# Token lists built by bfloat16 one-hot products in place of float32 ones and scatters

## The chip, the cores and the metric

The kernel runs on one core of one Trainium2 chip. The metric is the device time of one execution in microseconds (us), the median of the runs shown. The program is one launch of four stages that follow one another: a selective-scan (Mamba) stage, an attention stage, a routing stage and an expert stage.

## The reference

`x` has 16 sequences of 1,024 tokens of width 256, so 16,384 tokens. A Mamba block and an attention block come first; the last part is a mixture of experts, and it is what the change touches:

```python
probs = jax.nn.softmax(x.astype(jnp.float32) @ router_weight, axis=-1)   # 8 experts
top_p, top_i = jax.lax.top_k(probs, TOP_K)                                # TOP_K = 2
top_p = top_p / jnp.sum(top_p, -1, keepdims=True)
flat_exp = top_i.reshape(-1)
order = jnp.argsort(flat_exp)
...
keep = within < cap                                                       # cap = 5120
...
act = jax.nn.gelu(jnp.einsum('ech,ehf->ecf', exp_in, moe_w1), approximate=False)
exp_out = jnp.einsum('ecf,efh->ech', act, moe_w2).reshape(N_EXP * cap, H)
weighted = exp_out * padded_probs[:, None].astype(exp_out.dtype)
moe = jnp.zeros((N, H), exp_out.dtype).at[padded_ids].add(weighted)
```

Each token goes to its two best experts, and the two results are added to it with the two normalised probabilities as weights.

## The kernel before, in words

**Mamba and attention stages.** They take the first 4,386 us. The attention stage writes two results to DRAM that matter here: `n2`, the normalised rows of all tokens (16,384 rows of 256 float32), which SyncE stores in 64 parts of 256 KB, and `logits`, 8 numbers per token.

**Routing stage** (`routing_stage`, lines 1359 to 1592). Tokens lie as 128 tiles of 128 (one token per partition), so one instruction over all tokens and experts has 128 x 1024 elements. After the softmax, VectorE picks the two best experts as masks `best0` and `best1`, TensorE counts the tokens ahead of each (`within`, `total`), and VectorE makes from this the slot of each of the 256 entries (128 tiles times 2 choices) of each partition. VectorE's instructions up to there are a strict chain: the helper `after_last` makes each wait for the one before. Experts are cut into blocks of 256 slots; there is room for `NB` = 135 blocks, so 34,560 slots in `COLS` = 270 columns of 128 lanes. A slot is thus a lane and a column.

The list that says which token (and with which weight) sits in each slot is made in two ways at once:

- Of the 256 entries, 96 (`BY_POOL`) are scattered by GpSimd to a DRAM list `info` with one indirect DMA each (line 1456), 128 slots at a time. Entries past an expert's capacity get a slot out of bounds (`kept`), and are dropped.
- The other 160 (`BY_MATMUL`) are placed by TensorE. For an entry VectorE makes `hot_lane`, a 128 x 128 float32 matrix with the token number (z = 0) or the weight (z = 1) of partition p at its lane, and `hot_column`, 128 x 270, with a 1 at its column. The product of the two adds the entry into the bank `list_bank`:

```python
for n, (k, tile) in enumerate(BY_MATMUL):
    wait(dve, placed, n - HOT_RING + 1)
    ...
    for z in range(2):
        nc.vector.tensor_scalar(hot_lane[:, at, z], lane_f[:], place[:, k, tile:tile + 1], entry[:, k, tile, z:z + 1],
                                ALU.is_equal, ALU.mult)
    nc.vector.tensor_scalar(hot_column[:, at], column_f[:], column[:, k, tile:tile + 1], None,
                            ALU.is_equal).then_inc(hot, 1)
```

`HOT_RING` = 4 entries may be under way between VectorE and TensorE. When all are placed, ScalarE copies the bank to `made` (line 1467), and the stage ends with a barrier of all engines.

**Expert stage** (`expert_stage`, lines 1595 to 1781). SyncE loads `info` back as `listing`; GpSimd clears `xe` (so that vacant slots hold zeros) and makes the identity `ident`; VectorE adds `made`, and turns vacant slots into row numbers past the end (`token`, lines 1716 to 1728). Then 135 blocks run. For block n, GpSimd gathers 256 rows of `n2` by two indirect DMAs into `xe` (line 1659) and the expert's two weight matrices by two more (line 1651, 1 MB each, rows named by `weight_row`), TensorE transposes the rows (line 1746), multiplies by `w1` (line 1759) and by `w2` (line 1768), ScalarE applies GELU (line 1708), VectorE multiplies with the weight `listing[:, col, 1:2]` (line 1734), and GpSimd adds the rows into `out` by two indirect DMAs (line 1668). Weights and rows are loaded two blocks ahead.

## Time and profile before

| what | value |
| --- | --- |
| median of 3 runs | 6549.09 us (6548.19 to 6552.92) |
| the profiled execution | 6549.9 us |
| its span, first to last instruction | 6548.2 us |
| mean granted TensorE clock over the span | 0.976 of full |
| TensorE matmul busy | 6175.3 us (94%) |
| VectorE busy | 4267.1 us (65%) |
| ScalarE busy | 3519.6 us (54%) |
| GpSimd busy | 5132.0 us (78%) |

The table is of one execution. Busy time is the time in which an engine runs an instruction; it says nothing of whether another engine waits for it. Times of day in the rows further down count from the start of the span, and the granted clock is given as a share of 2.4 GHz.

### The profile page before, as it was taken

To read this page: it belongs to the slowest core of one execution; us is meant where nothing else is said; L and a number is where in the kernel's file an instruction comes from. 1 tells how busy PE (TensorE), PEld (TensorE's weight loads), DVE (VectorE), ACT (ScalarE), POOL (GpSimd) and SP (SyncE) were. 2 spreads that over 40 slices of the span, in tenths; PEclk is the share of its full clock that TensorE was granted. 3 is DMA by queue.
4 is the path that set the end of the run, shared out by engine and by line. 5 is a ranking of instruction groups with operands and counts; after the bars stand their busy time and mean duration, and the time that the engine had idled before them with its cause. 6 is when DMAs were issued, how large, how long until landed. Compare 5 with 4: busy or idle time off the path is not lost. (4 is left out here: it accounts for less than half of the span.)

```text
span 6548.2 us, 78761 instructions
## 1 busy us (share of the span) xinstructions
PE 6175.3 (94%) x25444; PEld 3970.3 (61%) x25444; DVE 4267.1 (65%) x5490; ACT 3519.6 (54%) x6418; POOL 5132.0 (78%) x3926
## 2 busy tenths in 40 slices
PE   7999999999999999999998799978999999999999
PEld 3444444444444444444443588866788888888888
DVE  6999999999999999999999377779100000000000
ACT  5677677767676777676766588750222222222222
POOL 6999999999999999999999677736454545454544
PEclk9999999999999999999999999989999999999999
DMA  3555555555555555555555244330566656566554
GB/s 124 166 162 171 166 168 166 168 165 168 165 172 163 166 165 166 170 164 169 166 163 167 62 121 122 116 120 1 175 190 179 190 179 189 180 189 179 183 162 135
DMA packets 551754, 1029.76 MB, mean 157 GB/s; under 512 B 77426, under 2 KB 245876, under 8 KB 516784
## 3 DMA queue, kind: packets, MB, share of 16 engines
q1 hardware_dynamic: 441168, 669.34, 33.3%
q0 software_dynamic: 110176, 355.39, 18.0%
q8 instruction: 204, 3.34, 0.2%
q14 instruction: 206, 1.69, 0.1%
HBM read 926.04 MB, written 88.72 MB: 155 GB/s over the span
## 5 line engine op out<-in xcount | busy, mean ns | idle before, releaser
L361 POOL TENSOR_TENSOR m_dbu<-m_du,m_bb 128x1024 f32<-128x1024 f32 x1024 | 2390.8, 2363 | 0.0
L739 PE MATMUL m_y_bank<-m_prod,m_ident 128*128 128x512 f32 x4096 | 1977.8, 612 | 143.1 <-POOL m_prod L370 143.1
L512 ACT ACTIVATE m_decay<-m_delta,m_a_neg 128x512 f32<-128x512 f32 x2048 | 1419.4, 695 | 724.7 <-DVE m_h L622 722.7
L739 PEld LDWEIGHTS m_y_bank<-m_prod,m_ident 128*128 128x128 f32 x4096 | 789.2, 196 | 1122.9 <-issue 907.2
L1734 DVE TENSOR_SCALAR e_ye<-e_ybank,e_listing 128x256 f32<-128x256 f32 x270 | 118.2, 479 | 1817.1 <-PE e_ybank L1768 1817.1
L622 DVE TENSOR_TENSOR_SCAN m_h<-m_decay,m_h_end,m_dbu 128x512 f32<-128x512 f32 x1024 | 1259.4, 1267 | 3.4 <-ACT m_decay L512 2.5
L622 DVE TENSOR_TENSOR_SCAN m_h<-m_decay,m_dbu 128x512 f32<-128x512 f32 x1024 | 1197.7, 1207 | 13.8 <-ACT m_decay L512 13.2
L1708 ACT ACTIVATE e_a<-e_ubank 128x512 f32<-128x512 f32 x540 | 322.5, 597 | 1473.6 <-PE e_ubank L1759 1473.6
L370 POOL TENSOR_TENSOR m_prod<-m_h,m_cb 128x1024 f32<-128x1024 f32 x416 | 982.5, 2362 | 20.0 <-issue 15.0
L1759 PE MATMUL e_ubank<-e_xT,e_w 128*128 128x256 f32 x4320 | 978.6, 380 | 1.3 <-ACT e_xT L1699 1.3
L1768 PE MATMUL e_ybank<-e_w,e_a 128*128 128x256 f32 x4320 | 954.5, 379 | 0.7 <-ACT e_a L1708 0.7
L1768 PEld LDWEIGHTS e_ybank<-e_w,e_a 128*128 128x128 f32 x4320 | 820.7, 190 | 112.6 <-ACT e_a L1708 1.1
L1651 POOL DMA_INDIRECT e_w<-in_w,weight_row x270 | 258.3, 957 | 799.0 <-PE e_ybank L1768 734.4
L1759 PEld LDWEIGHTS e_ubank<-e_xT,e_w 128*128 128x128 f32 x4320 | 811.6, 190 | 106.7 <-issue 1.6
L604 DVE TENSOR_TENSOR m_prod<-m_h,m_c_bank 128x1024 f32<-128x1024 f32 x608 | 727.3, 1196 | 42.5 <-ACT m_c_bank L499 22.4
L1668 POOL DMA_INDIRECT out<-e_ye,e_token x270 | 429.2, 1590 | 111.0 <-issue 81.3
L706 PE MATMUL m_side<-m_xnT,m_w_in 128*128 128x512 f32 x1024 | 503.0, 600 | 6.0 <-ACT m_xnT L428 6.0
L711 PE MATMUL m_side<-m_xpad,m_tap_diag 128*128 128x512 f32 x1024 | 495.7, 592 | 0.0
L499 ACT COPY m_c_bank<-m_cv 128x512 f32<-128x512 f32 x608 | 359.3, 591 | 95.3 <-DVE m_prod L604 93.1
L706 PEld LDWEIGHTS m_side<-m_xnT,m_w_in 128*128 128x128 f32 x1024 | 198.9, 195 | 260.3 <-issue 258.1
L1659 POOL DMA_INDIRECT e_xe<-n,e_token x270 | 283.8, 1051 | 85.4 <-issue 82.0
L711 PEld LDWEIGHTS m_side<-m_xpad,m_tap_diag 128*128 128x128 f32 x1024 | 194.3, 190 | 245.3 <-issue 245.3
(216 smaller groups left out, 6663.9 us busy)
## 6 DMA issues: line engine op xcount, KB each, us to landing
m_bb<-rows_bc SPq DMA_DIRECT2D x1024, 256.0 KB, 3.8
m_cv<-rows_bc SPq DMA_DIRECT2D x608, 256.0 KB, 4.0
m_cb<-rows_bc SPq DMA_DIRECT2D x416, 256.0 KB, 3.4
m_xin<-in_x SPq DMA_DIRECT2D x32, 512.0 KB, 5.7
m_xres<-in_x SPq DMA_DIRECT2D x32, 512.0 KB, 5.6
x<-m_xres SPq DMA_DIRECT2D x32, 512.0 KB, 6.3
a_xa<-x SPq DMA_DIRECT2D x64, 256.0 KB, 2.9
a_xr<-x SPq DMA_DIRECT2D x64, 256.0 KB, 3.2
```

Of the source, the lines that this page charges most:

```text
L361: nc.gpsimd.tensor_tensor(dbu[:, slot], du[:, q[1], p * PC:(p + 1) * PC], bb[:, slot].unsqueeze(1).to_broadcast([P, PC, T]), ALU.mult).the ...
L370: nc.gpsimd.tensor_tensor(prod[:, slot], h[:, slot], cb[:, C_BUFFER[k]].unsqueeze(1).to_broadcast([P, PC, T]), ALU.mult).then_inc(prod_by_ ...
L499: nc.scalar.copy(c_bank[:], cv[:, V_BUFFER[k]]).then_inc(c_copied, 1)
L512: nc.scalar.activation(decay[:, cc], delta[:, r, c], ACT.Exp, scale=a_neg[:, c, n:n + 1]).then_inc(decay_done, 1)
L604: nc.vector.tensor_tensor(prod[:, slot], h[:, slot], c_bank[:].unsqueeze(1).to_broadcast([P, PC, T]), ALU.mult).then_inc(prod_by_vector, 1)
L622: nc.vector.tensor_tensor_scan(h[:, slot, cc], decay[:, cc], dbu[:, slot, cc], h_end[:, u, cc:cc + 1] if r else 0.0, ALU.mult, ALU.add).th ...
L706: ins = nc.tensor.matmul(bank, w_in[:, piece, col:col + P], xnT[:, piece], start=(piece == 0), stop=final)
L711: ins = nc.tensor.matmul(bank, tap_diag[:, i, piece], xpad[:, i, piece:piece + T], start=(piece == 0), stop=final)
L739: ins = nc.tensor.matmul(y_bank[:, cc], ident[:], prod[:, slot, cc], start=False, stop=(n == NS - 1))
L1668: nc.gpsimd.indirect_dma_start(out, bass.IndirectOffsetOnAxis(ap=token[:, col:col + 1], axis=0), ye[:, n % Y_RING, j], None, compute_op=AL ...
L1759: ins = nc.tensor.matmul(ubank[:, (n * UG + g) % U_RING, i], w1[:, r, k, c * P:(c + 1) * P], xT[:, n % 2, k], start=(k == 0), stop=(k == K ...
L1768: ins = nc.tensor.matmul(ybank[:, n % 2, j], a[:, n % 2, c, j * P:(j + 1) * P], w2[:, n % W_RING, c], start=(c == 0), stop=(c == FC - 1))
```

## The change

All 256 entries are now placed by TensorE; the scatters, the DRAM list `info`, its clearing and its loading back are gone, and with them `kept` and `made`.

The entries go in 32 groups of 8 (4 tiles, both choices). Per group, VectorE makes 8 lane matrices in one instruction of 128 x 1024 elements in bfloat16 (`hot_lane`, a plain 0 or 1); ScalarE multiplies them by the partition number into `hot_row`; 8 column matrices of 128 x 270 in bfloat16 hold tile + 1 at the column (`hot_column`), and are made by VectorE in even groups and by GpSimd in odd ones. TensorE multiplies each column matrix by both, 16 products per group. One result is the tile + 1, the other the partition number times tile + 1, and VectorE gets the token number from them in 7 instructions after the last product. A ring of 4 groups lies between the engines.

The weights of the list are gone. `n2` gets rows of 260 numbers (`ROW`): the 256 values, the two probabilities and the two marks of the token's experts (8 minus the expert's number); the last four are stored by SyncE during the routing stage, 16 bytes per token. In the expert stage VectorE compares the marks of the gathered rows with that of the block's expert (`mark_of`) and so picks the probability (`match`, `share`), two small instructions per block.

The tiles of the expert stage that can be made early (`Shared`: `w1`, `w2`, `xe`, `ident`, `ln2`) are now alive in the routing stage. GpSimd clears `xe` and makes `ident` at its beginning, and issues the weight loads of blocks 0 and 1 at its end. The computation of `weight_row` moves from before the entries to behind group 4.

The diff, cut to its core:

```diff
-        n2_b = n2.rearrange("(s b p) m -> b p s m", s=S, p=P)
+        n2_b = n2[:, 0:H].rearrange("(s b p) m -> b p s m", s=S, p=P)
...
+def load_expert(nc, w, shared, n):
+    r = n % W_RING
+    for dst, src in ((shared.w1, w["w1"]), (shared.w2, w["w2"])):
+        nc.gpsimd.indirect_dma_start(
+            dst[:, r].rearrange("p k f -> p (k f)"), None, src,
+            bass.IndirectOffsetOnAxis(ap=shared.weight_row[:, n:n + 1], axis=0)).then_inc(shared.w_loaded[r], 16)
...
-def routing_stage(nc, logits, info, weight_row, made):
+def routing_stage(nc, w, logits, n2, shared):
...
+        def columns(eng, g, made):
+            at = g % HOT_RING
+            for j in range(EACH):
+                tile, k = g * SPAN + j // TOPK, j % TOPK
+                ins = eng.tensor_scalar(hot_column[:, at, j], column_h[:], column_of[:, tile, k:k + 1], float(tile + 1),
+                                        ALU.is_equal, ALU.mult)
+            ins.then_inc(made, 1)
...
-            sp.dma_start(info.rearrange("(p c) z -> p (c z)", p=P), empty[:].rearrange("p c z -> p (c z)")).then_inc(emptied, 16)
+            sp.dma_start(shared.ln2[:], w["ln_vecs"]).then_inc(shared.ln_loaded, 16)
+            sp.wait_ge(gates_made, 2)
+            sp.dma_start(n2[:, H:ROW].rearrange("(t p) z -> p t z", p=P),
+                         gate[:].rearrange("p t z k -> p t (z k)")).then_inc(gates_stored, 16)
+            sp.wait_ge(gates_stored, 16)
...
-            for n, (k, tile) in enumerate(BY_POOL):
...
-                nc.gpsimd.indirect_dma_start(
-                    info, bass.IndirectOffsetOnAxis(ap=slot_of[:, k, tile:tile + 1], axis=0),
...
+            pool.wait_ge(located, 1)
+            for g in BY_POOL:
+                wait(pool, placed, g - HOT_RING + 1)
+                columns(nc.gpsimd, g, column_by_pool)
+                if g == BY_POOL[-2]:
+                    pool.wait_ge(rows_made, 1)
+                    load_expert(nc, w, shared, 0)
+            load_expert(nc, w, shared, 1)
...
-            nc.scalar.copy(made[:].rearrange("p c z -> p z c"), list_bank[:, :, 0:COLS])
+            for g in range(GROUPS):
+                act.wait_ge(lane_made, g + 1)
+                wait(act, placed, g - HOT_RING + 1)
+                nc.scalar.activation(hot_row[:, g % HOT_RING], hot_lane[:, g % HOT_RING], ACT.Identity,
+                                     scale=row_f[:]).then_inc(row_made, 1)
...
+                for j in range(EACH):
+                    for z, of in enumerate((hot_row, hot_lane)):
+                        ins = nc.tensor.matmul(list_bank[:, z, 0:COLS], of[:, at, j], hot_column[:, at, j],
+                                               start=(g == 0 and j == 0), stop=(g == GROUPS - 1 and j == EACH - 1))
...
             for k in range(TOPK):
-                after_last(tt(prob[:], best[k][:], work[:], ALU.mult))
-                after_last(nc.vector.reduce_sum(kept[:, k], prob[:], axis=AXX))
                 after_last(tt(prob[:], best[k][:], rank[:], ALU.mult))
...
+            for g in range(GROUPS):
+                at = g % HOT_RING
+                tiles = slice(g * SPAN, (g + 1) * SPAN)
+                wait(dve, placed, g - HOT_RING + 1)
+                tt(hot_lane[:, at], lane_h[:].unsqueeze(1).to_broadcast([P, EACH, P]),
+                   lane_of_h[:, tiles].rearrange("p t k -> p (t k)").unsqueeze(2).to_broadcast([P, EACH, P]),
+                   ALU.is_equal).then_inc(lane_made, 1)
+                if g in BY_VECTOR:
+                    columns(nc.vector, g, column_by_vector)
+                if g == WEIGHTS_AT:
...
+                    nc.vector.tensor_copy(shared.weight_row[:], expert_f[:]).then_inc(rows_made, 1)
...
             def gather_rows(n):
                 wait(pool, t_made, n - X_RING + 1)
+                wait(pool, weighted, 2 * (n - X_RING + 1))
...
             for n in range(NB):
+                wait(dve, x_loaded[n % X_RING], turns(n, X_RING, J))
...
                 wait(dve, y_made, n + 1)
                 wait(dve, added, 16 * J * (n - Y_RING + 1))
                 for j in range(J):
-                    ins = nc.vector.tensor_scalar(ye[:, n % Y_RING, j], ybank[:, n % 2, j], listing[:, col, 1:2], None, ALU.mult)
+                    ins = nc.vector.tensor_scalar(ye[:, n % Y_RING, j], ybank[:, n % 2, j], share[:, n % 2, j:j + 1], None,
+                                                  ALU.mult)
```

VectorE where the slots are done, before. `r_` marks tiles of the routing stage; 128x270 is the shape that is written:

```order
L1577 CAST r_slot_of<-r_slot_f 128x256
L1578 TENSOR_TENSOR r_passed_e<-r_blocks_to,r_block_f 128x1080
L1580 TENSOR_REDUCE r_expert_f<-r_passed_e 128x135
L1581 TENSOR_SCALAR r_expert_f<-r_expert_f 128x135
L1582 TENSOR_SCALAR r_expert_f<-r_expert_f,r_row_f 128x135
L1583 CAST weight_row<-r_expert_f 128x135
L1589 TENSOR_SCALAR r_hot_lane<-r_lane_f,r_place,r_entry 128x128 x2
L1591 TENSOR_SCALAR r_hot_column<-r_column_f,r_column 128x270
L1589 TENSOR_SCALAR r_hot_lane<-r_lane_f,r_place,r_entry 128x128 x2
L1591 TENSOR_SCALAR r_hot_column<-r_column_f,r_column 128x270
```

And with the change, the same place:

```order
L1626 TENSOR_SCALAR r_column_of<-r_column_of 128x256
L1633 TENSOR_TENSOR r_hot_lane<-r_lane_h,r_lane_of_h 128x1024
L1470 TENSOR_SCALAR r_hot_column<-r_column_h,r_column_of 128x270 x8
L1633 TENSOR_TENSOR r_hot_lane<-r_lane_h,r_lane_of_h 128x1024 x2
L1470 TENSOR_SCALAR r_hot_column<-r_column_h,r_column_of 128x270 x8
L1633 TENSOR_TENSOR r_hot_lane<-r_lane_h,r_lane_of_h 128x1024 x2
L1470 TENSOR_SCALAR r_hot_column<-r_column_h,r_column_of 128x270 x8
```

The five instructions that make `weight_row` no longer stand ahead of the first lane matrix; they follow the columns of group 4. In an even group VectorE has one wide instruction and 8 columns for 8 entries, in an odd group the wide instruction alone (so `x2` is that of an odd group and that of the next even one).

GpSimd from the end of the slots to the first gather of the expert stage (`e_xe`), before:

```order
L1456 DMA info<-r_entry,r_slot_of 34560x2 x96
L1370 UNCONDITIONAL_BRANCH
L1645 UNCONDITIONAL_BRANCH
L1651 DMA e_w<-in_w,weight_row 128x2048 x2
L1673 IOTA e_dump_i 128x2
L1674 MEMSET e_xe 128x1536
L1675 MEMSET e_ident 128x128
L1677 AFFINE_SELECT e_ident<-e_ident 128x128
L1659 DMA e_xe<-n,e_token 128x256 x2
L1651 DMA e_w<-in_w,weight_row 128x2048 x2
L1659 DMA e_xe<-n,e_token 128x256 x4
```

And with the change, where `s_` marks the shared tiles:

```order
L1470 TENSOR_SCALAR r_hot_column<-r_column_h,r_column_of 128x270 x120
L1384 DMA s_w<-in_w,s_weight_row 128x2048 x2
L1470 TENSOR_SCALAR r_hot_column<-r_column_h,r_column_of 128x270 x8
L1384 DMA s_w<-in_w,s_weight_row 128x2048 x2
L1404 UNCONDITIONAL_BRANCH
L1693 UNCONDITIONAL_BRANCH
L1704 DMA s_xe<-n,s_token 128x260 x6
L1384 DMA s_w<-in_w,s_weight_row 128x2048 x2
L1704 DMA s_xe<-n,s_token 128x260 x2
```

The 96 scatters are replaced by 128 column instructions; the weight loads of two blocks stand ahead of the gathers and in the routing stage, the first of them between the last two groups of columns.

## Rows read from the trace of the kernel before

**Rows 1.** Page, slices of 164 us: busy tenths of TensorE; its granted clock in tenths.

```profile
PE   7999999999999999999998799978999999999999
...
PEclk9999999999999999999999999989999999999999
```

**Rows 2.** Windows; columns: stretch, us, busy us (instructions) per engine, granted clock, DMA share, GB/s.

```profile
4446.70:4596.00 149.30, 148.18 (x640) 122.76 (x640) 141.18 (x480) 0.03 (x1) 99.54 (x94) 0.98 0.02 1
...
4617.00:6510.00 1893.00, 1893.00 (x9033) 1666.66 (x9032) 115.60 (x264) 439.17 (x798) 951.11 (x793) 1.00 0.60 181
```

**Rows 3.** Timeline of VectorE's chain; columns: start, duration, engine, line, operation, tiles.

```profile
4391.75 0.69 DVE L1518 COPY r_prob<-r_raw 128x1024 f32<-128x1024 f32 x1
...
4415.07 0.95 DVE L1539 RECIPROCAL r_line<-r_line 128x128 f32<-128x128 f32 x1
...
4429.02 1.23 DVE L1560 TENSOR_TENSOR r_prob<-r_best,r_work 128x1024 f32<-128x1024 f32 x1
4430.27 1.22 DVE L1561 TENSOR_REDUCE r_kept<-r_prob 128x128 f32<-128x1024 f32 x1
...
4439.07 0.29 DVE L1564 CAST r_slot_of<-r_slot_f 128x256 int32<-128x256 f32 x1
...
4443.08 1.27 DVE L1578 TENSOR_TENSOR r_passed_e<-r_blocks_to,r_block_f 128x1080 f32<-128x1080 f32 x1
...
4446.74 0.60 DVE L1589 TENSOR_SCALAR r_hot_lane<-r_lane_f,r_place,r_entry 128x128 f32<-128x128 f32 x2
...
4447.52 0.60 DVE L1589 TENSOR_SCALAR r_hot_lane<-r_lane_f,r_place,r_entry 128x128 f32<-128x128 f32 x2
```

**Rows 4.** Groups by line, 4447 to 4596 us; columns as in part 5 of the page.

```profile
L1483 PE MATMUL r_list_bank<-r_hot_column,r_hot_lane 128*128 128x270 f32 x640 | 148.2, 395 | 27.4 <-DVE r_hot_column L1591 27.4
L1591 DVE TENSOR_SCALAR r_hot_column<-r_column_f,r_column 128x270 f32<-128x270 f32 x160 | 61.5, 385 | 0.0
```

**Rows 5.** Groups by line and shape, whole span: GpSimd, and TensorE at 512 columns.

```profile
L361 POOL TENSOR_TENSOR m_dbu<-m_du,m_bb 128x1024 f32<-128x1024 f32 x1024 | 2390.8, 2363 | 0.0
...
L739 PE MATMUL m_y_bank<-m_prod,m_ident 128*128 128x512 f32 x4096 | 1977.8, 612 | 143.1 <-POOL m_prod L370 143.1
...
L1261 PE MATMUL a_score<-a_causal,a_rows_of 16*32 16x512 bf16 x256 | 25.2, 384 | 0.0
...
L988 POOL TENSOR_SCALAR_AFFINE_SELECT a_causal<-a_causal 16x512 bf16<-16x512 bf16 x1 | 0.8, 839 | 0.0
```

**Rows 6.** Timeline of VectorE and GpSimd in the attention stage, 4100 to 4116 us.

```profile
4102.94 0.18 POOL L1005 TENSOR_TENSOR a_tmp<-a_moments,a_eps 128x2 f32<-128x2 f32 x1
...
4102.99 1.29 DVE L1217 TENSOR_SCALAR a_n<-a_hid,a_moments,a_rs 128x256 f32<-128x256 f32 x2
...
4103.35 0.96 POOL L1007 TENSOR_TENSOR a_rs<-a_tmp,a_minus_half 128x2 f32<-128x2 f32 x1
...
4105.51 0.69 POOL L1013 TENSOR_TENSOR a_rr<-a_tmp,a_minus_half 128x2 f32<-128x2 f32 x1
```

**Rows 7.** Timeline, 4370 to 4388 us: line 1217 with GpSimd idle.

```profile
4372.26 0.73 DVE L1217 TENSOR_SCALAR a_n<-a_hid,a_moments,a_rs 128x256 f32<-128x256 f32 x2 [1.08 <-POOL a_rs L1022]
```

**Rows 8.** Timeline from the last entry to the first transposes.

```profile
4595.97 0.63 ACT L1467 COPY made<-r_list_bank 128x540 f32<-128x540 f32 x1 [199.93 <-PEq L1487]
...
4597.62 1.01 POOL L1651 DMA_INDIRECT e_w<-in_w,weight_row  x1 [22.79 <-POOLq L1370]
...
4604.34 0.30 DVE L1728 CAST e_token<-e_token_f 128x270 int32<-128x270 f32 x1
4605.42 1.05 POOL L1659 DMA_INDIRECT e_xe<-n,e_token  x1 [3.45 <-DVE e_token L1728]
...
4609.81 1.09 PE L1746 MATMUL e_tbank<-e_ident,e_xe 128*128 128x128 f32 x4 [13.97 <-DMA e_xe<-n,e_token]
```

**Rows 9.** DMA issues over the span: size, median us from issue to landing.

```profile
e_xe<-n,e_token POOLq DMA_INDIRECT x270, 4.1
...
r_raw<-logits SPq DMA_DIRECT2D x1, 512.0 KB, 5.1
```

More of the change, by code:

```diff
@@ L1796, in build @@
     attention_stage(nc, x1, t, out, n2, logits)
[L1797 to L1799 removed]
+    with ExitStack() as ctx:
+        shared = Shared(nc, ctx)
+        routing_stage(nc, t, logits, n2, shared)
+        expert_stage(nc, t, n2, shared, out)
 def kernel(**inputs):
```

269 lines of the change are left out of this document (121 added, 148 removed).

## The prediction

> **What bounds the kernel now.** I first read the page's slices [rows 1]: TensorE is 0.9 busy nearly everywhere, at full clock, and the one dip, slice 28 of 40, is the end of attention and the routing stage. The rest of the work is not touched by the change. The windows then cut the end of the kernel [rows 2]. From 4617 to 6510 us, in the expert stage, TensorE is busy 1893.00 of 1893.00 us, so what else is added there on VectorE or GpSimd is beside TensorE and costs nothing until it makes TensorE wait. The stretch in which the list is made, 4446.7 to 4596.0, is 149.3 us, and TensorE is busy 148.2 of it. So before the change TensorE itself sets that pace: its 640 records there, two per float32 product, are 149.3 / 640 = 0.233 us apart [rows 2, 4]. The 96 scatters run beside it and end earlier (GpSimd is busy 99.5 us).
>
> In front of that stretch stands a strict chain on VectorE from the landing of the logits at 4391.75 to the first lane matrix at 4446.74, 55.0 us [rows 3]. Behind it, from ScalarE's copy at 4595.97 to the first transpose at 4609.81, 13.8 us pass in which TensorE has nothing to do [rows 8]. These three stretches, 218 us, are all that can become shorter.
>
> **The change, part by part.**
>
> *Ahead of the list.* A link of the chain on all tokens and experts costs 1.23 us and about 0.03 to the next [rows 3]. Four such go (`kept`): -5.0. One is added (`rank` plus `work`): +1.3. Eleven small links from 4439.07 to 4443.08, 4.0 us, become six: -2.0. The five of `weight_row`, 4443.08 to 4446.74, move behind group 4: -3.7 here. The reciprocal of 0.95 us now stands ahead of TensorE's counting, where it ran beside it: +1.0 [rows 3]. Nine casts and clearings ran while the logits were landing (issue to landing 5.1 us [rows 9]), so leaving them out gains nothing; six casts now stand beside ScalarE's exponential and reach past it a little, +0.4. Sum: -8.0. GpSimd's clearing of `xe` and the making of `ident` lie beside the landing and the first steps of the chain: nothing.
>
> *The list.* I count per pair of groups (one of VectorE, one of GpSimd), 16 entries, of which there are 16.
>
> - TensorE: 32 products of 270 columns. A float32 record of 512 columns lasts 612 ns, a bfloat16 one 384 ns [rows 5]: 228 ns less, about half of what a float32 record streams (0.233 us per record of 270 columns is two steps per column at 2.4 GHz). So a bfloat16 product of 270 columns takes 0.115 us, 3.7 us per pair, 59 us in all. The other end is that it takes as long as a float32 record, 0.23: 7.4 per pair.
> - ScalarE: two activations of 128x1024. They are beside the rest; it does little else in this stretch.
> - VectorE: two wide comparisons and 8 columns. The wide one has two inputs of 1024 elements. Ends: 0.69 us (the copy of as many elements with one input) and 1.23 (the product with two) [rows 3]. I take 1.15, the two-input row, less what free instructions overlap. A column now: three instructions between 4446.74 and 4447.52, 0.26 each [rows 3]; in bfloat16 between that and the part that doesn't shrink, 0.15; I take 0.20. Together 2 x 1.15 + 8 x 0.20 = 3.9 us.
> - GpSimd: 8 columns, an operation which the trace does not show. Ends: the mask of 512 bfloat16 elements, 0.839 us, gives 0.44 for 270 in proportion, and the two-input product, 2.363 us for 1024, gives 0.62 [rows 5]. One input: I take 0.44, 3.5 us per pair.
>
> If these ran freely, the slowest would set the pace at 3.9 us per pair. **They will not run freely.** In the attention stage two instructions of line 1217 (one input, 256 elements) take 0.73 us with GpSimd idle [rows 7] and 1.29 us when GpSimd works beside them, and GpSimd's operation of line 1007 takes 0.96 where its like on line 1013 takes 0.69 [rows 6]. VectorE's pair from 4102.99 and GpSimd's three (0.18, one more of 0.18, 0.96) end together at 4104.3. The work would be 0.73 + 0.18 + 0.18 + 0.69 = 1.78 us alone and takes 1.37: 0.77 of the sum, not the longer of the two. All of VectorE's instructions in the list are of such kinds, from SBUF to SBUF. So a pair takes (3.9 + 3.5) x 0.77 = 5.7 us, above TensorE's 3.7, and 16 pairs 91 us. Around them: 2 us from the first wide comparison to the first product; about 1.5 us for the weight loads of block 0, 1.0 us each and a gap on GpSimd [rows 8], which now stand before the last group's columns and are half hidden; 1.8 us for the last 16 products; and 1.7 of the 3.7 us of `weight_row`, in which GpSimd has the memory to itself. The list takes 98 us in place of 149.2: -51.2.
>
> The Trainium skill says of this in "SBUF — State Buffer", Who interferes with whom, that VectorE in a two-port mode, or with two SBUF inputs against a GpSimd operation that reads, and GpSimd lock one another out for the whole instruction. By it the sum of the two would count in full, which is a rival below; the rows show 0.77 of it. The skill's "VectorE: DVE Perf Modes", perf-mode tier table, gives a two-input bfloat16 operation double rate; that would be 0.5 us less each, 2 x 0.5 x 0.77 x 16 = 12 us. But the skill's "Vector Engine (DVE) Microarchitecture Reference", section 5.1, reports single rate where one input repeats one element, as the second one does here. No row here shows either.
>
> *Behind the list.* ScalarE's copy, the barrier, the loading of `info` and seven small instructions give way to seven small instructions on 270 columns, one a reciprocal (0.95 us for 128 elements [rows 3], so about 1.8): 4.7 us, the barrier 1.0 (the copy's end, 4596.60, to GpSimd's next work at 4597.62), then the gather. From the gather's issue to the transposes stay 4.4 us [rows 8]. That is 10.1 in place of 13.8. The weights of blocks 0 and 1, 4 MB, may still be landing when the gather is issued (median 4.1 us [rows 9]), for which I take 1.2 off: -2.5.
>
> *The expert stage.* Two instructions on 4 and 2 elements per block stand before VectorE's wait for the result, in which it is idle. GpSimd's new wait on them comes after it waited for VectorE's previous result anyway. Rows of 1,040 bytes for 1,024: the gather is issued two blocks ahead. Nothing. *The probabilities' store*: 16,384 pieces of 16 bytes. It must end before the barrier, over 100 us after its issue; nothing, with a rival below. *Attention*: rows of `n2` at another pitch; nothing, at most some 5 us.
>
> Sum: -8.0 - 51.2 - 2.5 = -61.7, against 6549.9 us of the profiled execution 6488.2. The median shown lies 0.8 lower: **6487 us**.
>
> **The rivals.**
>
> - *Free engines.* VectorE and GpSimd do not hinder one another with these shapes: 16 x 3.9 + 3.7 + 4 = 70 us, 28 less, 6459. For it: GpSimd works long and VectorE beside it in the Mamba stage. Against: rows 6.
> - *Full exclusion*: 16 x 7.4 + 6 = 124 us, 26 more, 6513. For it: the direction of rows 6.
> - *Slow columns or slow products.* GpSimd's columns at the two-input rate, 0.62 each, with full exclusion: 16 x 8.9 + 6 = 148, 6537. Or TensorE at 1.2 GHz, since it now pauses between groups, or products no faster than float32 records: 16 x 7.4 + 3 = 121, 6510.
> - *The other side: GpSimd's comparison is worked off slowly.* Its operation of line 1013 takes 0.69 us for 2 elements where line 1005 takes 0.18 [rows 6], so the operation matters there. GpSimd has 128 columns; from (149.2 + 10.5) / 128 = 1.25 us each the gain is gone, beyond 1.35 the kernel is slower by more than can be told from none. At 2 us each the list is 256 + 5 us and the kernel 6651. For it only line 1013, whose power is another matter; the mask, which compares as well, is quick [rows 5].
> - *It does not get what it is made for*: the list is quick, but the 16-byte store holds the barrier. It has about 115 us; 1,024 pieces on each of 16 queues would need over 0.11 us each. At 0.15 the end is 39 us late, 6526.
>
> **How the numbers follow.** My forecast gets 0.47, the free engines 0.20, full exclusion 0.13, slow columns or products 0.12, the store 0.03, the other side 0.05. About 0.2%, 13 us, is what can be told from no change. Of the slow cases a small part comes within that. Faster 0.92, same 0.03, slower 0.05. The range from 6458 to 6518 takes in the free engines, the forecast and full exclusion, and leaves out the slowest of the rest.
>
> **What would show it.** Right: the list about 98 us between the first wide comparison and the last product; TensorE's granted clock full but its busy share near 0.65; columns on VectorE longer than 0.3 us beside GpSimd's and short alone; TensorE busy all through the expert stage; the wide comparison near 1.2 us. Wrong: GpSimd's columns over 1 us; TensorE's idle time ended by ScalarE or by its own clock; the barrier ended by SyncE; the first transposes waiting for DMA more than 6 us after the gather is issued.

## The result, and the profile after

The changed kernel takes 6574.84 us (median of 6 runs, 6571.67 to 6577.78) where the kernel before takes 6550.14 in the same series: a ratio of 1.0038, 95% interval 1.0027 to 1.0048. It is slower by about 25 us. The forecast was 6487, so the sum was wrong by 88 us, and the rival "on the other side" came true.

The profiled execution took 6576.5 us, its span is 6574.7, 26.5 more than before. The page's slices of 164 us (busy tenths by engine, then TensorE's granted clock), beside [rows 1]:

```profile
PE   7999999999999999999998799965899999999999
...
DVE  6999999999999999999999377774000000000000
...
POOL 6999999999999999999999677739554545555454
PEclk9999999999999999999999999986999999999999
```

TensorE's dip has grown from 7 and 8 in slices 27 and 28 to 6, 5 and 8 in slices 27 to 29, and GpSimd stands at 9 in slice 28, in which the list is made. The windows of that stretch (stretch, us, then busy us and instructions per engine, granted clock, DMA share, GB/s) answer to [rows 2]:

```profile
4439.66:4619.56 179.90, 103.98 (x512) 68.86 (x512) 75.42 (x166) 36.71 (x32) 173.81 (x132) 0.66 0.04 16
4480.00:4520.00 40.00, 24.40 (x124) 16.29 (x122) 16.52 (x34) 8.52 (x8) 39.07 (x31) 0.71 0.00 0
4520.00:4560.00 40.00, 25.93 (x128) 17.30 (x128) 17.19 (x39) 8.70 (x8) 39.68 (x32) 0.66 0.00 1
4560.00:4600.00 40.00, 25.73 (x128) 17.28 (x128) 17.43 (x40) 9.19 (x8) 39.72 (x32) 0.66 0.00 1
```

From the first wide comparison to VectorE's first reading of the bank pass 179.9 us, against 149.3. GpSimd is busy 39.7 of 40 us, VectorE 17.3 and TensorE 25.8. The engine that was to be the helper is full, and the two that it was to relieve wait. The groups by line say for what (busy us, mean ns of one, idle us before it and who ended it), beside [rows 4]:

```profile
L1470 POOL TENSOR_SCALAR r_hot_column<-r_column_h,r_column_of 128x270 bf16<-128x270 bf16 x128 | 169.8, 1339 | 52.1 <-DVEq L1627 48.6
L1544 PE MATMUL r_list_bank<-r_hot_column,r_hot_row 128*128 128x270 bf16 x256 | 98.3, 393 | 93.0 <-POOL r_hot_column L1470 72.4 <-DVE r_hot_column L1470 20.6
L1544 PE MATMUL r_list_bank<-r_hot_column,r_hot_lane 128*128 128x270 bf16 x256 | 97.7, 392 | 0.0
L1633 DVE TENSOR_TENSOR r_hot_lane<-r_lane_h,r_lane_of_h 128x1024 bf16<-128x1024 bf16 x32 | 39.0, 1224 | 83.6 <-PE r_list_bank L1544 83.5
L1520 ACT ACTIVATE r_hot_row<-r_hot_lane,r_row_f 128x1024 bf16<-128x1024 bf16 x32 | 36.7, 1148 | 167.7 <-DVE r_hot_lane L1633 167.7
```

One column on GpSimd takes 1.339 us; its 128 columns are 170 of the 180 us. GpSimd itself waits only once, for the list to begin (48.6 us). TensorE waits 72.4 us for GpSimd's columns, and VectorE 83.5 us for TensorE to free a ring place, that is in the end for GpSimd too. GpSimd's line alone (min/median/max ns) and VectorE's on the same operation:

```profile
L1470 POOL TENSOR_SCALAR r_hot_column<-r_column_h,r_column_of x128: 1186/1196/2784, 4439.7 to 4614.3; 128x270 bf16<-128x270 bf16 x128
L1470 DVE TENSOR_SCALAR r_hot_column<-r_column_h,r_column_of x128: 161/281/521, 4440.8 to 4593.0; 128x270 bf16<-128x270 bf16 x128
```

Nearly all of GpSimd's cost is there without any disturbance: the median is 1.196 us. What other work adds is (1.339 - 1.196) x 128 = 18.3 us. The timeline shows how:

```profile
4494.52 1.20 POOL L1470 TENSOR_SCALAR r_hot_column<-r_column_h,r_column_of 128x270 bf16<-128x270 bf16 x1
4494.85 1.23 DVE L1633 TENSOR_TENSOR r_hot_lane<-r_lane_h,r_lane_of_h 128x1024 bf16<-128x1024 bf16 x1 [6.81 <-PE r_list_bank L1544]
4495.69 1.45 POOL L1470 TENSOR_SCALAR r_hot_column<-r_column_h,r_column_of 128x270 bf16<-128x270 bf16 x1
...
4498.39 1.63 POOL L1470 TENSOR_SCALAR r_hot_column<-r_column_h,r_column_of 128x270 bf16<-128x270 bf16 x1
4498.83 2.18 DVE L1470 TENSOR_SCALAR r_hot_column<-r_column_h,r_column_of 128x270 bf16<-128x270 bf16 x8
```

The first column was already running when the wide comparison began, and neither was lengthened. The second began 0.39 us before the comparison's end and took 0.25 us more. Over all columns it is so: the 28 that begin inside a wide comparison take longer by the rest of it, less about 0.1 us (two of them ran into the next comparison as well, 2.78 us), and so do 3 that began up to 0.05 us before one (2.23 to 2.25 us). All other comparisons began at least 0.34 us into a running column, or before the first one.

The other stretches went nearly as forecast. Behind the list:

```profile
4619.56 0.44 DVE L1648 TENSOR_SCALAR r_whole<-r_list_bank 128x270 f32<-128x270 f32 x1 [20.85 <-PEq L1548]
4620.03 1.84 DVE L1649 RECIPROCAL r_whole<-r_whole 128x270 f32<-128x270 f32 x1
...
4625.80 1.03 POOL L1704 DMA_INDIRECT s_xe<-n,s_token  x1 [7.86 <-SPq L1668]
4630.03 1.12 PE L1774 MATMUL e_tbank<-s_ident,s_xe 128*128 128x128 f32 x4 [10.60 <-DMA s_xe<-n,s_token]
```

So the span's 26.5 us are these, between events that both traces have [rows 3, 8]:

| stretch | before | after | difference |
|---|---|---|---|
| start to first wide comparison (first lane matrix) | 4446.74 | 4439.66 | -7.1 |
| from there to the bank's first reader | 149.2 | 179.9 | +30.7 |
| bank's first reader to first transposes | 13.8 | 10.5 | -3.4 |
| first transposes to last scatter's issue | 1932.3 | 1932.4 | +0.1 |
| last scatter's issue to the end of the span | 6.1 | 12.3 | +6.2 |

The last line is a surprise. GpSimd's last DRAIN (the instruction with which it closes the stage, in the trace the last thing it does) takes 7,972 ns in place of 1,838.

The list's 179.9 us are 171.4 of columns, 2.6 for the issue of block 0's weight loads between the last two groups, 4.0 from the last column to VectorE's reading of the bank, in which TensorE makes its last 16 products, and 1.9 of small gaps.

### The profile page after: what moved, and what is told of

The parts are those of the page before. It is cut to its first block and busy times, and to the rows that moved or that the text cites. A ratio compares the mean times of both kernels' runs of the same rounds, so it can differ in the third digit from the quotient of the medians.

```text
span 6574.7 us, 78602 instructions
## 1 busy us (share of the span) xinstructions
PE 6132.4 (93%) x25316; PEld 3917.7 (60%) x25316; DVE 4231.4 (64%) x5430; ACT 3553.6 (54%) x6449; POOL 5201.0 (79%) x3956
## 3 DMA queue, kind: packets, MB, share of 16 engines
q14 instruction: 206, 1.69, 0.1%
## 5 line engine op out<-in xcount | busy, mean ns | idle before, releaser
L1763 DVE TENSOR_SCALAR e_ye<-e_ybank,e_share 128x256 f32<-128x256 f32 x270 | 118.2, 479 | 1768.7 <-PE e_ybank L1796 1768.7
L1787 PE MATMUL e_ubank<-e_xT,s_w 128*128 128x256 f32 x4320 | 978.8, 380 | 1.3 <-ACT e_xT L1735 1.3
L1796 PE MATMUL e_ybank<-s_w,e_a 128*128 128x256 f32 x4320 | 954.5, 379 | 0.7 <-ACT e_a L1744 0.7
L1796 PEld LDWEIGHTS e_ybank<-s_w,e_a 128*128 128x128 f32 x4320 | 820.9, 190 | 112.4 <-ACT e_a L1744 1.1
L1787 PEld LDWEIGHTS e_ubank<-e_xT,s_w 128*128 128x128 f32 x4320 | 812.0, 190 | 106.6 <-issue 1.6
L1384 POOL DMA_INDIRECT s_w<-in_w,s_weight_row x270 | 259.7, 962 | 777.2 <-PE e_ybank L1796 735.5
L1713 POOL DMA_INDIRECT out<-e_ye,s_token x270 | 430.4, 1594 | 111.1 <-issue 81.4
L1704 POOL DMA_INDIRECT s_xe<-n,s_token x270 | 282.5, 1046 | 90.1 <-issue 82.3
```

The lines of the kernel that those rows point to most:

```text
L1713: nc.gpsimd.indirect_dma_start(out, bass.IndirectOffsetOnAxis(ap=token[:, col:col + 1], axis=0), ye[:, n % Y_RING, j], None, compute_op=AL ...
L1787: ins = nc.tensor.matmul(ubank[:, (n * UG + g) % U_RING, i], w1[:, r, k, c * P:(c + 1) * P], xT[:, n % 2, k], start=(k == 0), stop=(k == K ...
L1796: ins = nc.tensor.matmul(ybank[:, n % 2, j], a[:, n % 2, c, j * P:(j + 1) * P], w2[:, n % W_RING, c], start=(c == 0), stop=(c == FC - 1))
```

## The experiments

**Who sets the list.** The first two kernels change which groups' columns GpSimd makes. In e1_all_vector, where it makes none, it issues all four weight loads as soon as their rows are made.

```diff
-    BY_POOL = [g for g in range(GROUPS) if g % 2]
+    BY_POOL = []                                    # e1_all_vector
+    BY_POOL = [g for g in range(GROUPS) if g % 4 == 1]   # e2_pool_quarter
```

> All 32 groups of columns are made by VectorE; GpSimd only issues the weight loads of blocks 0 and 1 early. Theory A (GpSimd's column, 1.196 us at best and 1.34 us on average, sets the pace of the list: 128 of them are 171 us): the list falls from 179.8 us to VectorE's own 32 x (1.15 + 2.0) = 101 us plus 3.7 for the weight rows and 4 at the ends, about 109, the kernel to about 6504. Theory B (TensorE at 1.2 GHz sets it: 32 x 3.6 = 115 us of products): about 120 us of list, 6515, unless its clock rises, and VectorE waits for it. Theory C (the loss sits in the store of the probabilities or in the early weight loads): no change from 6575. The last DRAIN of GpSimd, 8.0 us in the changed kernel and 1.8 before, goes back to 1.8 if it comes from GpSimd having run tensor_scalar in the list, and stays if it comes from anything else of the change.

Measured: 6486.91 us, ratio to the kernel before 0.9903 (0.9886 to 0.9919). This is 88 us faster than the change. Theory A has the cause right and its price too high: it expected a list of 109 us and 6504. Theories B and C are out. GpSimd's last DRAIN stays at 7,972 ns, so it isn't the columns on GpSimd that made it long. The groups:

```profile
L1540 PE MATMUL r_list_bank<-r_hot_column,r_hot_row 128*128 128x270 bf16 x256 | 63.2, 286 | 43.7 <-DVE r_hot_column L1470 43.7
L1470 DVE TENSOR_SCALAR r_hot_column<-r_column_h,r_column_of 128x270 bf16<-128x270 bf16 x256 | 53.9, 281 | 0.0
L1629 DVE TENSOR_TENSOR r_hot_lane<-r_lane_h,r_lane_of_h 128x1024 bf16<-128x1024 bf16 x32 | 38.8, 1211 | 0.1
```

VectorE has no idle time before either line now, so the list is VectorE's sum: a group takes 2.73 us, 1.21 for the wide comparison and 1.68 for eight columns with 0.16 of overlap, and the list 93.6 us.

> GpSimd makes the columns of every fourth group (8 of 32), VectorE those of 24. Theory A: GpSimd has 64 columns of about 1.3 to 1.5 us, 90 us, VectorE 32 x 1.15 + 24 x 2.0 = 85 us, so a list of 95 to 100 us and a kernel near 6495, 80 us less than the change. Theory B: 120 us of list, TensorE without idle time. If GpSimd's columns get slower with more of VectorE's work beside them (mean over 1.6 us), the list is over 105.

Measured: 6535.69 us, ratio 0.9977 (0.9968 to 0.9987). No theory came near; only the last condition held (mean over 1.6 us, list over 105).

```profile
L1470 POOL TENSOR_SCALAR r_hot_column<-r_column_h,r_column_of 128x270 bf16<-128x270 bf16 x64 | 102.8, 1617 | 74.4 <-DVEq L1627 48.5 <-PE r_list_bank L1544 24.4
```

The list takes 139.3 us. With 0, 64 and 128 of the 256 columns on GpSimd it takes 93.6, 139.3 and 179.9: each column that is given to GpSimd costs 0.6 to 0.7 us, and neither share gains. Here GpSimd isn't busy all the time. With a ring of four and every fourth group its own, it may begin a group only when its last one has been placed, so its 13.1 us of columns and TensorE's 16 products after them stand in series (group 5's products end at 4475.42, GpSimd begins group 9 at 4475.52): the 24.4 us of waiting. These 16 products take 3.3 to 3.8 us, at the lower clock, against 2.0 for later groups at full clock, so in this kernel the lower clock does cost time, some 10 us over seven turns (an estimate). A longer ring was not tried.

**What a column costs GpSimd, and why.** e3_probe is e1_all_vector with pairs of small operations put into GpSimd's idle time in the expert stage, nothing left out:

```diff
+                lambda: nc.gpsimd.tensor_scalar(p_bo[:], p_bf[:], p_s[:], 3.0, EQ, MU),
...
+                lambda: nc.gpsimd.tensor_scalar(p_fo[:], p_f[:], 2.0, 3.0, MU, AD),
...
+                lambda: nc.gpsimd.tensor_tensor(p_fo[:], p_f[:], p_f[:], MU),
```

> As the kernel with all columns on VectorE, and GpSimd runs, in its idle time in the expert stage, eight forms of 270 elements, twice in a row and twice over: is_equal with a pointer then mult in bfloat16 (the form of the columns) and in float32; is_equal alone; mult alone in bfloat16 and in float32; mult and add with constants; the column's form on 135 elements; a product of two inputs. Theory A1 (the comparison is what is slow): the forms with is_equal take 1.2 us, the others under 0.5. Theory A2 (the second operation is): forms with two operations 1.2, with one about 0.5. Theory A3 (any tensor_scalar costs GpSimd 4.4 ns an element): all 1.2, 135 elements 0.65. The two-input product in the Mamba stage takes 2.36 us for 1024, so 0.65 for 270 is expected of it under all three.

Measured, in a single run of 6489.14 us (min/median/max ns; the minimum is that of a pair's second instruction, the maximum that of its first, which stands right behind the issue of a scatter of line 1715):

```profile
L1726 POOL TENSOR_SCALAR e_p_bo<-e_p_bf,e_p_s x4: 1197/1500/1809, 4782.7 to 5240.7; 128x270 bf16<-128x270 bf16 x4
L1727 POOL TENSOR_SCALAR e_p_fo<-e_p_f,e_p_s x4: 1197/1494/1800, 4839.7 to 5297.7; 128x270 f32<-128x270 f32 x4
L1728 POOL TENSOR_SCALAR e_p_bo<-e_p_bf,e_p_s x4: 961/1254/1555, 4896.7 to 5354.5; 128x270 bf16<-128x270 bf16 x4
L1730 POOL TENSOR_SCALAR e_p_fo<-e_p_f x4: 892/1204/1515, 5010.7 to 5468.4; 128x270 f32<-128x270 f32 x4
L1731 POOL TENSOR_SCALAR e_p_fo<-e_p_f x4: 423/714/1023, 5067.8 to 5524.9; 128x270 f32<-128x270 f32 x4
L1732 POOL TENSOR_SCALAR e_p_bo<-e_p_bf,e_p_s x4: 760/1071/1402, 5124.8 to 5582.4; 128x135 bf16<-128x135 bf16 x4
L1733 POOL TENSOR_TENSOR e_p_fo<-e_p_f x4: 636/918/1206, 5181.8 to 5639.1; 128x270 f32<-128x270 f32 x4
```

The column's form takes 1.197 us with nobody beside it, so its price is its own. bfloat16 saves nothing on GpSimd (L1726, L1727). Half the elements take 0.760, so an element costs (1197 - 760) / 135 = 3.2 ns and the rest is 0.32 us. The comparison is not what is dear: a lone multiplication takes 0.89 and a lone comparison 0.96 (L1730, L1728). A multiplication followed by an addition takes 0.423, less than the multiplication alone, and a product of two tensors 0.636. None of the three theories holds; only the 0.65 us for the two-input product came true. GpSimd's time goes by the form of the instruction, with more than a factor of two between forms of one size.

**Is it GpSimd even when VectorE is quick?** e6_entries_inside makes VectorE's wide comparison quicker; e11_change_inside is the change with that edit.

```diff
-        lane_h = sb("lane_h", [P, P], BF16)
+        lane_h = sb("lane_h", [P, P, EACH], BF16)
...
-        hot_lane = sb("hot_lane", [P, HOT_RING, EACH, P], BF16)
+        hot_lane = sb("hot_lane", [P, HOT_RING, P, EACH], BF16)
...
-                tt(hot_lane[:, at], lane_h[:].unsqueeze(1).to_broadcast([P, EACH, P]),
-                   lane_of_h[:, tiles].rearrange("p t k -> p (t k)").unsqueeze(2).to_broadcast([P, EACH, P]),
+                tt(hot_lane[:, at], lane_h[:],
+                   lane_of_h[:, tiles].rearrange("p t k -> p (t k)").unsqueeze(1).to_broadcast([P, P, EACH]),
```

> As e1_all_vector, but the eight one-hot rows of a group lie with the entry as the innermost dimension (lane outside), so that both inputs of VectorE's wide comparison have neighbouring bfloat16 elements innermost and neither repeats one element; TensorE then loads its weights with a stride of 16 bytes. It computes the same. Theory A (the repeated element is what holds the wide comparison at 1.21 us for 1,024 elements): it takes 0.6 to 0.75 us, a group 2.15 to 2.3 us instead of 2.73, the list 13 to 18 us less, 6469 to 6475. Theory B (a comparison of two inputs runs at 1.2 us in any layout): 6485 to 6489. Theory C (strided weights slow TensorE's loads, 16 of them a group): a product takes over 0.14 us instead of 0.116, TensorE becomes the bound at more than 2.2 us a group, and the gain is halved or gone.

Measured: 6470.96 us, ratio 0.9881 (0.9864 to 0.9897).

```profile
L1629 DVE TENSOR_TENSOR r_hot_lane<-r_lane_h,r_lane_of_h 128x1024 bf16<-128x1024 bf16 x32 | 21.7, 679 | 0.1
L1540 PEld LDWEIGHTS r_list_bank<-r_hot_column,r_hot_lane 128*128 128x128 bf16 x256 | 37.9, 148 | 1.2
```

The wide comparison falls from 1.211 to 0.679 us, the list from 93.6 to 76.6. TensorE's loads take 0.148 in place of 0.100 us, but its products are 0.117 to 0.119 us apart against 0.116: theory A, and C only as far as a cost that is hidden. The layout of both inputs changed: the one that repeated single elements now repeats a row of eight, and the one that repeated a row no longer repeats at all.

> The change (GpSimd makes the columns of the odd groups, 128 of 256) with e6_entries_inside's layout, which takes VectorE's wide comparison from 1.22 to 0.68 us and changes nothing else. In e6_entries_inside, where VectorE set the list, that was worth 16 us. Theory A (GpSimd sets the list: 8 columns of 1.20 us alone for each pair of groups, more where it stands behind VectorE's two-input instruction): the list is 128 x 1.20 = 154 us at the least, about 165 to 172 instead of 179.8, since a column beside a wide comparison waits 0.5 us instead of 1.05; 6560 to 6567, and VectorE's idle time in the list grows from 83 us to over 90. Theory B (VectorE or TensorE at its half clock sets it): the list becomes 16 to 17 us shorter or more, 6558 or less. Theory C (GpSimd's columns wait for VectorE's port in any case, 1.34 us each): no difference, 6575.

Measured: 6565.57 us, ratio 1.0023 (1.0014 to 1.0033).

```profile
L1470 POOL TENSOR_SCALAR r_hot_column<-r_column_h,r_column_of 128x270 bf16<-128x270 bf16 x128 | 160.3, 1266 | 51.9 <-DVEq L1627 48.3
L1633 DVE TENSOR_TENSOR r_hot_lane<-r_lane_h,r_lane_of_h 128x1024 bf16<-128x1024 bf16 x32 | 23.2, 728 | 90.7 <-PE r_list_bank L1544 90.5
```

VectorE has 16 us less to do in the list, and idles 90.5 us. The list takes 170.4 us, 9.5 less than the change; what GpSimd's columns lose to the comparison fell from 18.3 to 9.0 us, 9.3. That is theory A, and the contention is priced: 18 of 180 us in the change. TensorE's half clock can't be the pace in either kernel, since GpSimd's columns follow one another without a wait. The granted clock is 0.66 over the list in the change and 0.73 here, with TensorE idle for 93 us in each; in e1_all_vector, where it idles 43.7 us, it is 0.84 from 4440 to 4460 us, 0.97 in the next 20, and 1.00 in the 50 behind them.

This kernel also shows the other side of the contention, which the change had no occasion to show:

```profile
4476.37 1.20 POOL L1470 TENSOR_SCALAR r_hot_column<-r_column_h,r_column_of 128x270 bf16<-128x270 bf16 x1
4476.44 0.96 DVE L1633 TENSOR_TENSOR r_hot_lane<-r_lane_h,r_lane_of_h 128x1024 bf16<-128x1024 bf16 x1 [5.67 <-PE r_list_bank L1544]
```

The comparison begins 0.07 us into the column and takes 0.96 us in place of 0.69, while the column keeps its 1.20. Eight comparisons began 0.07 to 0.31 us into a column. Seven of them took 0.72 to 0.96 us and ended 1.03 us behind the column's start; at the eighth it was the column that waited (1.75). From 0.37 us on neither is lengthened. So a column holds a comparison too, but only in its first third of a microsecond.

**Is there a split that gains?** e10_one_column gives GpSimd one column of each group, which it has time for, on top of e8_late_behind (below).

```diff
+            for g in range(GROUPS):
                 wait(pool, placed, g - HOT_RING + 1)
+                columns(nc.gpsimd, g, column_by_pool, [EACH - 1])
...
+                columns(nc.vector, g, column_by_vector, range(EACH - 1))
```

> As e8_late_behind, with the split placed within a group: of a group's eight columns GpSimd makes one and VectorE seven. Theory A (GpSimd needs 1.2 us for it, up to 2.25 where VectorE's wide comparison runs beside it, which stays under a group's time of 2.2 us; VectorE isn't slowed): VectorE's group is 0.68 + 7 x 0.21 = 2.15 us instead of 2.36, the list 6 us less than in e8_late_behind, about 6459. Theory B (GpSimd's column, with the semaphore steps on either side, is slower than a group of VectorE): the list goes at 2.4 to 2.7 us a group, up to 10 us slower than e8_late_behind. Theory C (TensorE's 16 products of 0.116 us and the waits between engines set the group): no difference.

Measured: 6471.38 us, ratio 0.9882 (0.9866 to 0.9899); its base has 6470.91. The number is that of theory C, but the reason is another. VectorE in this kernel, and then in e6_entries_inside:

```profile
4493.63 0.68 DVE L1627 TENSOR_TENSOR r_hot_lane<-r_lane_h,r_lane_of_h 128x1024 bf16<-128x1024 bf16 x1
4494.23 1.67 DVE L1470 TENSOR_SCALAR r_hot_column<-r_column_h,r_column_of 128x270 bf16<-128x270 bf16 x7
4495.81 0.68 DVE L1627 TENSOR_TENSOR r_hot_lane<-r_lane_h,r_lane_of_h 128x1024 bf16<-128x1024 bf16 x1
```

```profile
4492.70 0.68 DVE L1629 TENSOR_TENSOR r_hot_lane<-r_lane_h,r_lane_of_h 128x1024 bf16<-128x1024 bf16 x1
4493.30 1.69 DVE L1470 TENSOR_SCALAR r_hot_column<-r_column_h,r_column_of 128x270 bf16<-128x270 bf16 x8
4494.90 0.68 DVE L1629 TENSOR_TENSOR r_hot_lane<-r_lane_h,r_lane_of_h 128x1024 bf16<-128x1024 bf16 x1
```

Beside GpSimd, VectorE's seven columns take 1.66 to 1.75 us, about what eight take alone; in the four groups that GpSimd did not touch they took 1.49. GpSimd does hinder VectorE's one-input instructions: what it took over, it cost.

**The end of the kernel.** Four kernels look for the 6.2 us. e4_before_wide_rows is the kernel before with the change's wider rows; e5_late_weights moves the first weight loads back.

```diff
-    n2 = scratch("n2", (TOKENS, H))
+    n2 = scratch("n2", (TOKENS, H + 4))          # e4_before_wide_rows
```

> The kernel before, with the change's rows alone: each row of n2 is 260 elements apart instead of 256 (4 zeros behind it, written as 16-byte pieces during the routing stage), and the expert stage gathers 260. List, scatters and gates are as before. It tests what the wide rows cost, and whether they are why GpSimd's last DRAIN took 7.97 us in the change and 1.84 in the kernel before. Theory A (wide rows do nothing by themselves): the time is within 0.1% of the kernel before (6550), a block of the expert stage stays at 14.25 us, the last DRAIN at 1.8 us. Theory B (the DRAIN goes with the wide rows or the gathers of 1,040 bytes): the last DRAIN is 8 us and the time 6556. Theory C (1,040-byte rows slow the gathers so that TensorE waits): a block costs more than 14.3 us, 132 blocks give 10 us or more.

Measured: 6550.76 us, ratio 1.0002 (0.9992 to 1.0013); the last DRAIN 1,838 ns. Theory A: the wide rows cost nothing, in the gathers as at the end.

```diff
-            load_expert(nc, w, shared, 0)
-            load_expert(nc, w, shared, 1)
...
+            load_weights(0)
             gather_rows(0)
+            load_weights(1)
             gather_rows(1)
```

> As e1_all_vector (every column on VectorE, 6486.9), but the weight loads of blocks 0 and 1 are issued in the expert stage behind the gathers, as in the kernel before; the routing stage then issues no indirect transfer at all. Theory A (early weight loads gain nothing, since the first block waits for the gathered rows, their transposes and ScalarE's copy, and the long last DRAIN has nothing to do with them): 6485 to 6489, DRAIN 8.0 us. Theory B (the long DRAIN comes from transfers issued in the stage ahead of the last one): DRAIN 1.8 us and 6481. Theory C (the first matmul waits for its weights): the first product of the expert stage starts 1.5 to 3 us later behind the first transposes, 6488 to 6490 unless B holds too.

As the diff shows, the loads in this kernel stand ahead of the gathers, not behind them as the expectation says; this is the kernel before's own order, where block 0's loads ran while VectorE made the token list [rows 8]. Measured: 6487.59 us, ratio 0.9903 (0.9886 to 0.9919), the DRAIN 1,849 ns. The end is 6.1 us shorter, and the time is that of e1_all_vector all the same, since the first transposes come 5.8 us later (4547.58 against 4541.73, list ends 0.2 apart): the first gather is issued 2.9 us later, behind the two loads, and takes 7.2 us to the transposes in place of 4.2. Theory A's time came true without its DRAIN, and B's DRAIN without its time; C is out, since the first product stands 2.4 us behind the first transposes in both kernels. e8_late_behind (on e6_entries_inside) sets them behind the gathers, which neither kernel did; e9_one_early leaves block 0's loads early and sets only block 1's behind.

```diff
             gather_rows(0)
+            load_weights(0)      # e8_late_behind only
             gather_rows(1)
+            load_weights(1)
```

> As e6_entries_inside (6471.0), with the weight loads of blocks 0 and 1 in the expert stage, each behind its block's gathers, as in the kernel before (in e5_late_weights, as built, each stood ahead of them, and the first transposes came 5.8 us later than in e1_all_vector). Theory A (GpSimd's last DRAIN is long when weight loads were issued in the stage ahead, and the order ahead of the gathers was what ate e5_late_weights' 6.1 us): DRAIN 1.8 us, first product as early as in e6_entries_inside behind the token list, 6464 to 6466. Theory B (the first product waits for its weights): up to 3 us of it are lost, 6466 to 6468.

Measured: 6470.91 us, ratio 0.9880 (0.9864 to 0.9896), the DRAIN 1,849 ns.

```profile
4534.95 5.68 PE L1782 MATMUL e_ubank<-e_xT,s_w 128*128 128x256 f32 x16 [5.94 <-DMA s_w<-in_w,s_weight_row]
```

In e6_entries_inside this first product waited 1.26 us, for ScalarE; here 5.94, for its weights. Theory B's mechanism at more than its price: 4.7 us, and most of the DRAIN's gain is gone again; the 1.6 us that should be left don't show in the time. So hiding block 0's loads ahead of the token list is worth 4.7 to 5.8 us in these kernels.

> As e6_entries_inside, with block 0's two weight loads in the routing stage and block 1's two in the expert stage, behind the gathers of blocks 0 and 1. It tells apart what the last DRAIN goes by. Theory A (any indirect transfer issued in the stage ahead makes it long): 8.0 us, 6471. Theory B (it goes with the number of transfers issued ahead, 6.1 us for four, so 1.5 us each): 4.9 us, 6468. Theory C (it hangs on the total of transfers in the last stage by a bound between 806 and 810, here 808): 1.8 us, 6465.

Measured: 6467.34 us, ratio 0.9876 (0.9860 to 0.9893), the DRAIN 1,847 ns. By the DRAIN only theory C agrees; the time can't tell C from B, and lies 3.6 us below e6_entries_inside where the end of the span became 6.3 us shorter. With 810 or 808 indirect transfers issued in the last stage the DRAIN is short, with 806 long. Of weight loads issued in the stage ahead, two leave it short and four do not, yet in the kernel before and in e4_before_wide_rows 96 scatters issued there leave it short too. So a mere number of transfers ahead isn't it; the total of the last stage, or the kind of those ahead, was not separated.

**The best version.** e12_rows_by_pool takes VectorE's six instructions for the weight rows out of the list.

```diff
+            for e in range(E - 1):
...
+                    own(nc.gpsimd.tensor_scalar(passed_e[:, :, 0], block_f[:], blocks_to[:, e:e + 1], None, ALU.is_ge))
+                    own(nc.gpsimd.tensor_tensor(expert_f[:], expert_f[:], passed_e[:, :, 0], ALU.add))
...
-                if g == WEIGHTS_AT:
```

> As e9_one_early (6467.3), with the six instructions that find each block's expert (4.6 us of VectorE, in the middle of the list) made by GpSimd instead, as eight comparisons, seven additions and three others of 135 elements, while it has nothing else to do; the weight loads wait for them. Theory A (the list is VectorE's sum, and what is taken from it comes off): the list 76.7 less 4.5 us, less what VectorE's columns are slowed by GpSimd beside them; 6463 to 6465. Theory B (GpSimd beside VectorE slows its columns, 0.24 for 0.19 us as in e10_one_column, for the 15 to 20 us that GpSimd works): 2 to 4 us of it come back, 6465 to 6468. Theory C (GpSimd's 18 instructions end so late that block 0's weights are waited for): over 6468.

Measured: 6463.84 us, ratio 0.9870 (0.9853 to 0.9886): theory A's time, but not for its reason. GpSimd needed 16 instructions, from 4436.18 to 4449.4 us. The list shrank by 0.3 us only, 76.7 to 76.4, since VectorE's columns beside them were slow:

```profile
4442.39 2.64 DVE L1470 TENSOR_SCALAR r_hot_column<-r_column_h,r_column_of 128x270 bf16<-128x270 bf16 x8
...
4451.04 1.69 DVE L1470 TENSOR_SCALAR r_hot_column<-r_column_h,r_column_of 128x270 bf16<-128x270 bf16 x8
```

Five groups lost 3.3 of the 3.6 us that a group had been longer by. That is theory B's mechanism, and within its price. The lead over e9_one_early isn't explained by the list; the runs of the two overlap (6462.68 to 6465.89, and 6464.35 to 6468.89), so the two can't be told apart.

## Why the prediction was wrong

- **The step that failed** is GpSimd's column in the part on the list: "the mask of 512 bfloat16 elements, 0.839 us, gives 0.44 for 270 in proportion ... One input: I take 0.44". It is 1.196 us undisturbed and 1.339 in the mean. Both ends of the bound were too low. They came from other operations [rows 5], scaled by elements, though one row at hand, 0.69 us for two elements against 0.18 [rows 6], said that the operation decides. e3_probe shows this: one size, 0.42 to 1.20 us by form. With 1.20 in place of 0.44 the prediction's own sum gives 16 x (3.9 + 9.6) x 0.77 + 7 = 173 us of list, so this one price is 75 of the 82 us by which the list was wrong.
- **The rival on the other side** gave the mechanism. By its own sum a column of 1.339 us makes the kernel 12 us slower, just short of what it said can be told from none. The rest of the span's 26.5 us is 8.5 in the list beside the columns (two load issues, the last 16 products, gaps) and 6.2 at the end, neither in its sum. It stood at 0.05. The profile had no row for this operation on GpSimd; a term on which 128 instructions hang and that no row prices should have had its rival at more than that, and the low end of the range had no claim to be so near.
- **The overlap by 0.77 of the sum** fell as a mechanism, though not by its number. Per pair of groups VectorE has 4.1 us of work alone (2 x 1.21 + 1.69) and GpSimd 9.6 (8 x 1.196); 0.77 of that sum is 10.5, and the pair took 10.3 in the steady part (4494.85 to 4505.21 and to 4515.51). That is chance. GpSimd alone is the pace, 39.7 of 40 us busy, and the rest is the wait of columns for a wide comparison, 18.3 us in the change, not a fraction of the sum. Where GpSimd has little to do the rule fails: in e10_one_column it gives (2.15 + 1.20) x 0.77 = 2.6 us a group, and the steady groups take 2.23. The Trainium skill, "SBUF — State Buffer", Who interferes with whom, says that the one that issues first holds the shared port and the other blocks fully. The traces agree for columns that begin inside a comparison. Where a comparison begins inside a column they agree only for the column's first 0.34 us (e11_change_inside); later in it both are as long as alone (4494.52 and 4494.85: 1.20 and 1.23 us).
- **VectorE's terms.** The wide comparison: 1.15 assumed, 1.22 measured. A column: 0.20 assumed, 0.21 measured alone (1.68 for eight) and 0.27 beside GpSimd (2.18). In e6_entries_inside, without the repeated element in one input, the comparison takes 0.68 us. That agrees with both rules cited of the Trainium skill, each for its layout: "Vector Engine (DVE) Microarchitecture Reference", 5.1, for the change's, and the tier table of "VectorE: DVE Perf Modes" for the other.
- **TensorE's term.** 0.115 us per product was right at full clock (0.116 apart in e1_all_vector). In the change the clock fell to the 1.2 GHz level for much of the list, products went 0.225 us apart there, and it cost nothing but in the last group (about 1.6 us), since TensorE waited 93 us anyway. The signs named ahead, "TensorE's granted clock full" for right and "GpSimd's columns over 1 us" for wrong, read correctly.
- **Ahead of the list**: -8.0 forecast, -7.1 measured. TensorE's counting products take 6.5 us from the first to VectorE's scan in place of 5.2: the granted clock is 0.50 for the first 4 us at least, where before it is 1.00 from 3.2 us on. These 1.3 us cover the difference.
- **Behind it**: -2.5 forecast, -3.4 measured; the first gather did not suffer from the weights, whose last load was issued 8.8 us ahead of it (4.2 us from its issue to the transposes, against 4.4).
- **The expert stage and the 16-byte store** at nothing: right (1932.3 and 1932.4 us; the store's 16,384 pieces landed 24.7 us after their issue at 4416.6, over 170 us ahead of the barrier).
- **The end of the kernel** was not looked at: +6.2 us from GpSimd's last DRAIN, the one term that was missing altogether. Its cause stays open.
- The prediction read one dip, in slice 28, out of [rows 1]; the row has 7 in slice 27 and 8 in slice 28. Nothing hangs on it.
- That 6487 is also the time of e1_all_vector is chance: that kernel's list is 93.6 us where 98 were forecast, by another division of the work.

## What to carry to other kernels

Before work is shared with GpSimd, find a row of that very form of instruction on GpSimd; where there is none, measure it, or hold the range open on the slow side, since the form of an instruction moves its price by more than a factor of two at one size. Here a column is 0.21 us on VectorE and 1.20 on GpSimd, and even the work that GpSimd had time for came back as longer instructions on VectorE (e10_one_column, e12_rows_by_pool). Look for the missing factor in the layout of the busy engine first: putting the entry innermost nearly halved the wide comparison and was worth 16 us, where none of the three splits tried gained anything. A transfer moved across a stage's boundary is judged by both ends: by the wait that it takes from the first product, and by what the stage's end then costs.

## What was not expected of the hardware

- GpSimd takes 0.42 us for multiply-then-add with constants, 0.89 for the multiplication alone, 1.20 for compare-then-multiply, all on 270 elements; the last two are the same in bfloat16 and float32.
- GpSimd's instruction right behind the issue of a scatter-add takes 0.6 us more (1.80 against 1.20, 1.02 against 0.42, in e3_probe). Behind the issue of a weight load it does not: in the change the column at 4605.99 took 1.22 us.
- GpSimd's column and VectorE's two-input comparison hold one another, but not for equally long: a column that begins inside a comparison waits for nearly all of its rest, a comparison that begins inside a column only until 0.34 us after the column's start. VectorE's one-input bfloat16 columns are lengthened beside GpSimd, eight from 1.69 to as much as 2.64 us.
- GpSimd's DRAIN at the end takes 1.84 or 7.97 us, by how the indirect transfers are spread over the last two stages. Why stays open.
